# Moving the bias of the last feed-forward layer from TensorE rows to a GpSimd add, with all output tiles on VectorE

## The chip, the cores and the metric

The kernel runs on one core of one Trainium2 chip. The metric is the device time of one execution in microseconds (us). The engines are TensorE (PE, with its weight loads PEld), VectorE (DVE), ScalarE (ACT), GpSimd (POOL) and SyncE (SP), which here issues the DMAs. SBUF is the on-chip memory, PSUM the accumulator banks that TensorE writes.

## The reference

A sandwich ("macaron") transformer layer on x of 8 x 1024 tokens with 256 features:

```python
x = x + 0.5 * ffn(layernorm(x))
x = x + attention(layernorm(x))
x = x + 0.5 * ffn(layernorm(x))
```

The attention is causal with 16 heads of 16 features. The feed-forward layer has 8 nominal experts that share one weight matrix; since each token goes to two slots of them and none overflows, its part of that matrix product is scaled with the sum of the two renormalised top gates:

```python
scores = softmax(xf @ W_gate)                 # 7 gates
expert_weights, _ = top_k(scores, 2)
expert_weights = expert_weights / expert_weights.sum(-1, keepdims=True)
...
shared = xf @ W_shared.T
out = (shared + moe_out + bias).reshape(b, n, d)
```

## The kernel before, in words

Three stages follow one another. Stage A does the first feed-forward layer and the q, k, v projections, stage B the attention, and stage C (`stage_c`, from L1326), which is the one changed, everything after it: the division of the attention numerators by the softmax sums, the output projection, the residual, the layer norm, and the last feed-forward layer with its gates. Matrix products keep float32 accuracy by splitting both operands into a high and a low part: each product of 256 x 256 is six matmuls (high x high, high x low, low x high, for two halves of the 256 features), written by the helper `project` (L148, matmuls recorded at L152).

Stage C works on 16 chunks of 512 tokens, four tiles of 128 tokens in each. The engines are programmed apart, each with its own order written out by hand, and meet at semaphores. Each has a function `step(c, ...)`; steps 0 to 3 (and the last) are written out, the others run in loops of two chunks a turn (`turns`). In step c:

- **TensorE**: output projection of tile 0 of chunk c, the eight transposes of the normalised chunk c-1 (L247), output projection of tiles 1 to 3 (L152), then `pe_tile` four times for chunk c-1: expert columns and gate logits (264 columns, L152), then the shared weights (256 columns, L1240). Ahead of the latter, one matmul (L1237) of a constant matrix of twos with a row matrix holding the halved bias adds the bias into PSUM.
- **ScalarE**: the high half `xh` of chunk c-1 out of the transposes (L254), the exponentials of the gates of chunk c-2 (L1261), the high half `oh` of chunk c+1 (L1450), `yl` of tiles 0 to 2 of chunk c-1 (L1251: half the expert product, with the logits), the normalisation `xn` of chunk c (four instructions, L237), `yl` of tile 3, and the scaling of tiles 2 and 3 of chunk c-2 with the gate sum (`act_scale`, L1256).
- **VectorE**: `acc` of the second half of chunk c-2 (`dve_collect`, L1268: PSUM x 0.5 + residual), the logits (`lmax` L1276, `dl` L1277), the low half `xl` of chunk c-1 (L259), residual and statistics of chunk c (L1492, L210, L218), the gates of chunk c-2 (L1287 to L1295), output tiles 0 and 1 of chunk c-2 (`dve_outs`, L1306: yl x gate sum + acc), `acc` of the first half of chunk c-1.
- **GpSimd**: output tiles 2 and 3 of chunk c-3 (`pool_outs`, L1314), the low half `ol` of chunk c+1 (L1415), mean and inverse deviation of chunk c (L225 to L229), the division for chunk c+2 (L1410).
- **SyncE**: loads of numerators and inverse sums of chunk c+3 (L427, L434), the store of chunk c-3 (L1323), the load of the residual of chunk c+2 (L438).

An instruction that waits holds up everything behind it on its engine. Two buffers each (`acc`, `yl`, `out`, `x2`, `oh`, `ol`) alternate by the parity of the chunk. Ahead of the first step VectorE builds the bias row and the twos in five instructions (L1523 to L1527). Stage A adds its bias on GpSimd, a tile at a time (L365, `a_ffn_xb`).

Of the kernel before, what the change touches and what calls it, by code (L numbers as in the profile page):

```python
# [26 lines left out]
P = 128  # L27
# [1162 lines left out]
class Tail:  # L1190


    SPLIT = 2

    def __init__(self, ar, name, w, banks, ln, bias_w):
        self.w, self.banks, self.ln, self.bias_w = w, banks, ln, bias_w
        sb, sem = (lambda n, s, d=F32: ar.sb(f"{name}_{n}", s, d)), (lambda n: ar.sem(f"{name}_{n}"))
        self.acc = [sb(f"acc{n}", [P, TPC, E]) for n in range(2)]
# [16 lines left out]
        self.scaled = sem("scaled")  # L1215
        self.dve_out_done = sem("dve_out_done")
        self.pool_out_done = sem("pool_out_done")
        self.stored = [sem(f"stored{n}") for n in range(2)]

    def pe_tile(self, pe, k, t, first):  # L1220
# [23 lines left out]
    def act_tile(self, act, k, t, turn, fresh):  # L1244
        act.wait_ge(self.ex_done, k * TPC + t + 1)
        if not fresh:
            if t < self.SPLIT:
                act.wait_ge(self.dve_out_done, (k - 2) * 2 + t + 1)
            else:
                act.wait_ge(self.pool_out_done, (k - 2) * 2 + t - 1)  # L1250
        act.mul(self.yl[turn][:, t, :], self.banks["X"][t % 2][:, 0:YL], 0.5).then_inc(self.yl_ready, 1)  # L1251

    def act_scale(self, act, k, turn):
        act.wait_ge(self.gate_chain, k * GATE_LINKS + GATE_LINKS)
        for t in range(self.SPLIT, TPC):
            act.activation(self.yl[turn][:, t, 0:E], self.yl[turn][:, t, 0:E], ACT.Identity, scale=self.wsum[:, t:t + 1],  # L1256
                           bias=self.ln.zero[:, 0:1]).then_inc(self.scaled, 1)
# [21 lines left out]
    def dve_gate(self, dve, k, prev_scaled):  # L1279
# [3 lines left out]
        if prev_scaled:  # L1283
            dve.wait_ge(self.scaled, k * 2)
# [41 lines left out]
def stage_c(nc, psum, const, io, scratch, chunk):  # L1326
    ident, mhalf, zero, hbias, wh, wl, hold = const
    with ExitStack() as ctx:
# [14 lines left out]
        bh = ar.sb("c_bh", [P, E], F32R)  # L1343
        bl = ar.sb("c_bl", [P, E])
        bt = ar.sb("c_bt", [P, E])
        brow = ar.sb("c_brow", [P, E], F32R)
        twos = ar.sb("c_twos", [P, P], F32R)
        ln = Ffn(ar, "c_ln", (wh, wl), banks, zero)
        ffn = Tail(ar, "c_ffn", (wh, wl), banks, ln, (twos, brow))
# [7 lines left out]
        bias_chain = ar.sem("c_bias_chain")  # L1357
# [6 lines left out]
        def _(sp):  # L1364
# [8 lines left out]
            def step(c, parity, o_next, out3, x_next):  # L1373
# [23 lines left out]
            ffn.store(sp, io, LAST, LAST % 2, last=True)  # L1397
# [4 lines left out]
        def _(pool):  # L1402
# [237 lines left out]
```

## Time and profile before

| | before |
|---|---|
| time, median of 3 runs | 1353.83 us (1350.99 to 1354.71) |
| the profiled execution: time | 1353.6 us |
| its span | 1351.8 us |
| mean granted TensorE clock | 0.963 of full speed |
| PE busy | 1245.0 us, 92%, 9324 matmuls |
| DVE busy | 1138.3 us, 84% |
| ACT busy | 920.7 us, 68% |
| POOL busy | 435.0 us, 32% |
| last stage (L1403 to the end) | from 1150 us on, some 200 us |

Busy shares are averages over the whole program. A row of the timeline has a start, a duration, engine, line, operation, the output tile and the inputs with their shapes, a count of merged instructions, and in brackets the engine's idle time before it and what ended that. Merged rows cover all their instructions, which overlap a little at their ends: two of 1.29 us together may be 0.60 us apart.

### The profile page before, as it was taken

What the parts mean: (1) busy time and instruction counts of PE and PEld (TensorE: products, weight loads), DVE (VectorE), ACT (ScalarE), POOL (GpSimd) and SP (SyncE); (2) the same over time, 40 slices, a digit from 0 to 9 for tenths busy, and PEclk for the clock granted to TensorE, in tenths of its full rate; (3) what the DMA queues carried; (4) which work ended last, traced back from release to release, by engine and by line L of the source; (5) the groups of instructions that cost most, each with busy time, mean ns of one, the idle gap of its engine ahead of it and who ended that gap; (6) DMA issues with size and microseconds to landing.
All of it is one profiled execution on the core that took longest, in us unless ns stands there. A gap on an engine that the chain in (4) does not pass through costs nothing. (4 is left out here: it accounts for less than half of the span.)

```text
span 1351.8 us, 37753 instructions
## 1 busy us (share of the span) xinstructions
PE 1245.0 (92%) x9324; PEld 825.8 (61%) x9324; DVE 1138.3 (84%) x4510; ACT 920.7 (68%) x1858; POOL 435.0 (32%) x843
## 2 busy tenths in 40 slices
PE   4999999978999999999999999999999997699996
PEld 3988888964554454554554554554554543599996
DVE  4788888749999999999999999999999994367775
ACT  3666666630777777777777777777777777356654
POOL 3333333301222222222222222222322322467772
PEclk9999999985899999999999999999999999699998
DMA  3366666881564564664664664664664663556651
GB/s 113 141 225 225 225 225 225 220 274 37 78 107 81 99 106 80 101 104 80 103 102 80 103 102 80 104 101 80 106 99 80 106 99 107 158 180 196 192 165 63
DMA packets 121900, 174.12 MB, mean 129 GB/s; under 512 B 44012, under 2 KB 71788, under 8 KB 121804
## 3 DMA queue, kind: packets, MB, share of 16 engines
q1 hardware_dynamic: 121816, 173.30, 56.4%
q14 instruction: 67, 0.55, 0.2%
q8 instruction: 17, 0.28, 0.1%
HBM read 96.08 MB, written 76.02 MB: 127 GB/s over the span
## 5 line engine op out<-in xcount | busy, mean ns | idle before, releaser
L1000 ACT ACTIVATE b_probs<-bank 128x512 f32<-128x512 f32 x1152 | 597.4, 612 | 135.4 <-PE bank L1124 131.6
L1027 DVE CUSTOM_DVE_ANT_0 b_junk<-bank,mask 128x512 bf16<-128x512 f32 (+3 forms) x1032 | 446.8, 488 | 1.4 <-issue 1.2
L1030 DVE TENSOR_REDUCE b_pm<-bank 128x1 f32<-128x512 f32 x516 | 322.4, 683 | 19.7 <-PE bank L1101 18.7
L1143 PE MATMUL bank<-b_probs,b_vx 128*32 128x512 f32 (+3 forms) x3072 | 310.3, 499 | 4.2 <-ACT b_o L985 1.9
L1124 PE MATMUL bank<-qs,ks 50*128 50x512 f32 (+3 forms) x1056 | 293.6, 383 | 4.3 <-ACT b_probs L1000 0.4
L1101 PE MATMUL bank<-ks,qs 48*128 48x512 f32 (+3 forms) x1056 | 277.2, 390 | 10.9 <-PEq L443 6.3
L1101 PEld LDWEIGHTS bank<-ks,qs 48*128 48x128 f32 x1056 | 165.1, 193 | 134.6 <-DVE b_pm L1030 61.5
L145 POOL TENSOR_TENSOR hold_pool<-zero 128x1 f32<-128x1 f32 x192 | 37.4, 195 | 629.9 <-ACT b_probs L1000 474.3
L1124 PEld LDWEIGHTS bank<-qs,ks 50*128 50x128 f32 x1056 | 159.7, 188 | 57.3 <-ACT b_probs L1000 52.4
L960 POOL TENSOR_SCALAR_AFFINE_SELECT b_probs<-b_probs 128x512 f32<-128x512 f32 x256 | 158.5, 638 | 0.0
L1143 PEld LDWEIGHTS bank<-b_probs,b_vx 128*32 128x32 f32 x3072 | 71.1, 109 | 109.6 <-issue 80.9
L1124 PE MATMUL bank<-b_qs,b_ks 50*128 50x512 f32 (+2 forms) x480 | 135.3, 379 | 2.0
L1101 PE MATMUL bank<-b_ks,b_qs 48*128 48x512 f32 (+2 forms) x492 | 123.1, 371 | 2.0 <-DVE b_pm L1027 2.0
L152 PE MATMUL bank<-wh,a_ln_xh 128*128 128x256 f32 (+1 forms) x384 | 114.5, 298 | 6.1 <-DVE a_ln_xl L259 6.1
L152 PE MATMUL bank<-wh,a_ln_xl 128*128 128x256 f32 (+1 forms) x384 | 110.7, 288 | 0.0
L152 PE MATMUL bank<-wl,a_ln_xh 128*128 128x256 f32 (+1 forms) x384 | 110.3, 287 | 0.0
L1101 PEld LDWEIGHTS bank<-b_ks,b_qs 48*128 48x128 f32 x492 | 74.2, 185 | 56.9 <-DVE b_pm L1030 28.0
L1124 PEld LDWEIGHTS bank<-b_qs,b_ks 50*128 50x128 f32 x480 | 73.8, 185 | 24.5 <-ACT b_probs L1000 22.6
L237 ACT ACTIVATE a_ln_xn<-a_x,a_ln_nbias,a_ln_rstd 128x256 f32<-128x256 f32 x128 | 72.2, 591 | 21.8 <-POOL a_ln_nbias L229 21.3
L1027 DVE DVE_READ_ACCUMULATOR2_ANT b_pm<- 128x1 f32 x1032 | 85.7, 83 | 0.0
L152 PEld LDWEIGHTS bank<-wh,a_ln_xh 128*128 128x128 f32 x384 | 75.1, 196 | 10.5 <-DVE a_ln_xl L259 4.8
L152 PEld LDWEIGHTS bank<-wl,a_ln_xh 128*128 128x128 f32 x384 | 75.0, 195 | 0.8
(120 smaller groups left out, 1993.8 us busy)
## 6 DMA issues: line engine op xcount, KB each, us to landing
scr_qk<-a_qk SPq DMA_DIRECT2D x64, 512.0 KB, 3.2
qs<-scr_qk SPq DMA_DIRECT2D x132, 128.0 KB, 4.5
ks<-scr_qk SPq DMA_DIRECT2D x132, 128.0 KB, 5.1
scr_o<-b_o SPq DMA_DIRECT2D x64, 256.0 KB, 3.7
b_qs<-scr_qk SPq DMA_DIRECT2D x66, 128.0 KB, 4.0
b_ks<-scr_qk SPq DMA_DIRECT2D x66, 128.0 KB, 4.6
a_x<-x SPq DMA_DIRECT2D x16, 512.0 KB, 3.5
scr_x<-a_x SPq DMA_DIRECT2D x16, 512.0 KB, 2.7
```

What stands on the lines that cost most here:

```text
L145: pool.tensor_tensor(self.pool_out[:, col:col + 1], zero[:, 0:1], zero[:, 1:2], ALU.add)
L152: last = pe.matmul(out, a, b, start=(n == 0), stop=(n == len(terms) - 1))
L237: act.activation(self.xn[:, t, :], x[:, t, :], ACT.Identity, scale=self.rstd[:, t:t + 1], bias=self.nbias[:, t:t + 1]).then_inc(self.xn_re ...
L960: ins = pool.affine_select(out=blk, in_=blk, compare_op=ALU.is_ge, fill=0.0, base=0, pattern=[[0, GH], [1, P]], channel_multiplier=-1)
L1000: act.activation(probs[:, PROB_BUF[s], h, :], score_bank(g, t, last)[:], ACT.Exp).then_inc(p_ready, 1)
L1027: ins = dve.tensor_tensor_reduce(junk[:, t % MB, off:off + w], src, mask[:, BANK - w:BANK], 1.0, 0.0, ALU.add, ALU.max, pm[:, g.buf, 0, pl ...
L1030: ins = dve.tensor_reduce(pm[:, g.buf, 1, place(h), i:i + 1], src, AX.X, ALU.max)
L1101: last = pe.matmul(m_bank[t % MB][:, off:off + w], qs[g.buf][rows(h, SROWS), h // 2, i * P:(i + 1) * P], ks[g.buf][rows(h, SROWS), h // 2, ...
L1124: done = pe.matmul(score_bank(g, t, last)[:, off:off + w], ks[g.buf][rows(h, SROWS_M), h // 2, j * P:(j + 1) * P], qs[g.buf][rows(h, SROWS ...
L1143: last = pe.matmul(o_bank[2 * D * h:2 * D * (h + 1), col:col + w], vx[g.buf][:, j, h, :], probs[:, PROB_BUF[src], h, off:off + w], start=( ...
```

## The change

The bias is no longer a matmul. GpSimd adds the halved bias to the residual stream of the chunk, two instructions of two tiles each (`pool_xb`), in step c between the inverse deviation and the division; `acc` reads that sum in place of x2. VectorE writes all four output tiles of a chunk, each with its gate sum, so that ScalarE's scaling and GpSimd's two output adds are gone. The store of chunk c-2 comes in step c (before: c-3), behind the residual load. The bias rows, the twos and their five instructions are gone.

```diff
-    SPLIT = 2
-
-    def __init__(self, ar, name, w, banks, ln, bias_w):
-        self.w, self.banks, self.ln, self.bias_w = w, banks, ln, bias_w
+    def __init__(self, ar, name, w, banks, ln, hbias):
+        self.w, self.banks, self.ln, self.hbias = w, banks, ln, hbias
         sb, sem = (lambda n, s, d=F32: ar.sb(f"{name}_{n}", s, d)), (lambda n: ar.sem(f"{name}_{n}"))
+        self.xb = [sb(f"xb{n}", [P, TPC, E]) for n in range(2)]
...
-        half = sh[:, t % 2 * E:(t % 2 + 1) * E]
-        twos, brow = self.bias_w
-        pe.matmul(half, twos[:], brow[:], start=True, stop=False)
-        terms = [(a[ch], b[:, ch, cols]) for ch in range(KC) for a, b in ((lh, wh), (lh, wl), (ll, wh))]
-        for i, (a, b) in enumerate(terms):
-            last = pe.matmul(half, a, b, start=False, stop=(i == len(terms) - 1))
+        last = project(pe, sh[:, t % 2 * E:(t % 2 + 1) * E], lh, ll, [wh[:, ch, cols] for ch in range(KC)],
+                       [wl[:, ch, cols] for ch in range(KC)])
...
         if not fresh:
-            if t < self.SPLIT:
-                act.wait_ge(self.dve_out_done, (k - 2) * 2 + t + 1)
-            else:
-                act.wait_ge(self.pool_out_done, (k - 2) * 2 + t - 1)
+            act.wait_ge(self.out_done, (k - 2) * TPC + t + 1)
...
-    def act_scale(self, act, k, turn):
-        act.wait_ge(self.gate_chain, k * GATE_LINKS + GATE_LINKS)
-        for t in range(self.SPLIT, TPC):
-            act.activation(self.yl[turn][:, t, 0:E], self.yl[turn][:, t, 0:E], ACT.Identity, scale=self.wsum[:, t:t + 1],
-                           bias=self.ln.zero[:, 0:1]).then_inc(self.scaled, 1)
...
-    def dve_collect(self, dve, k, p, x, turn, fresh):
+    def pool_xb(self, pool, k, x, turn, fresh):
+        if not fresh:
+            pool.wait_ge(self.acc_ready, k * 2 - 2)
+        for p in range(2):
+            two = slice(2 * p, 2 * p + 2)
+            pool.tensor_tensor(self.xb[turn][:, two, :], x[:, two, :], self.hbias[:].unsqueeze(1).to_broadcast([P, 2, E]),
+                               ALU.add).then_inc(self.xb_ready, 1)
+
+    def dve_collect(self, dve, k, p, turn):
         dve.wait_ge(self.sh_done, k * 2 + p + 1)
-        if p == 1 and not fresh:
-            dve.wait_ge(self.pool_out_done, (k - 1) * 2)
+        dve.wait_ge(self.xb_ready, k * 2 + p + 1)
         two = slice(2 * p, 2 * p + 2)
         dve.scalar_tensor_tensor(out=self.acc[turn][:, two, :].rearrange("p t e -> p (t e)"), in0=self.banks["S"][p][:], scalar=0.5,
-                                 in1=x[:, two, :].rearrange("p t e -> p (t e)"), op0=ALU.mult,
+                                 in1=self.xb[turn][:, two, :].rearrange("p t e -> p (t e)"), op0=ALU.mult,
...
-        if prev_scaled:
-            dve.wait_ge(self.scaled, k * 2)
...
-    def dve_outs(self, dve, k, turn, fresh, tiles):
+    def dve_outs(self, dve, k, turn, fresh):
         self.out_free(dve, k, turn, fresh)
-        dve.wait_ge(self.acc_ready, k * 2 + (1 if tiles[-1] < 2 else 2))
-        for t in tiles:
+        dve.wait_ge(self.acc_ready, k * 2 + 2)
+        for t in range(TPC):
             dve.scalar_tensor_tensor(out=self.out[turn][:, t, :], in0=self.yl[turn][:, t, 0:E], scalar=self.wsum[:, t:t + 1],
-                                     in1=self.acc[turn][:, t, :], op0=ALU.mult, op1=ALU.add).then_inc(self.dve_out_done, 1)
-
-    def pool_outs(self, pool, k, turn, fresh):
-        self.out_free(pool, k, turn, fresh)
-        pool.wait_ge(self.acc_ready, k * 2 + 2)
-        for t in range(self.SPLIT, TPC):
-            pool.wait_ge(self.scaled, k * 2 + t - 1)
-            pool.tensor_tensor(self.out[turn][:, t, :], self.yl[turn][:, t, 0:E], self.acc[turn][:, t, :],
-                               ALU.add).then_inc(self.pool_out_done, 1)
-
-    def store(self, sp, io, k, turn, last=False):
-        if last:
-            sp.wait_ge(self.dve_out_done, k * 2 + TPC)
-        else:
-            sp.wait_ge(self.dve_out_done, k * 2 + 2)
-            sp.wait_ge(self.pool_out_done, k * 2 + 2)
+                                     in1=self.acc[turn][:, t, :], op0=ALU.mult, op1=ALU.add).then_inc(self.out_done, 1)
+
+    def store(self, sp, io, k, turn):
+        sp.wait_ge(self.out_done, k * TPC + TPC)
...
-            def step(c, parity, o_next, out3, x_next):
+            def step(c, parity, o_next, out2, x_next):
                 if o_next:
                     sp.wait_ge(on_ready, c * KC + 2 * KC)
                     load_o(c + 3, 1 - parity)
-                if out3:
-                    ffn.store(sp, io, c - 3, 1 - parity)
                 if x_next:
                     sp.wait_ge(x2_ready, c * 2 + 2)
                     load_x1(c + 2, parity)
+                if out2:
+                    ffn.store(sp, io, c - 2, parity)
...
-            def step(c, parity, out3, nxt, nxt2, first=False):
-                if out3:
-                    ffn.pool_outs(pool, c - 3, 1 - parity, isinstance(c, int) and c < 5)
+            def step(c, parity, nxt, nxt2, first=False):
                 if nxt:
                     low(c + 1, 1 - parity)
                 ln.pool_rstd(pool, c, mhalf, first)
+                ffn.pool_xb(pool, c, x2[parity], parity, isinstance(c, int) and c < 2)
                 if nxt2:
                     divide(c + 2, parity)
...
-                if prev2:
-                    ffn.act_scale(act, c - 2, parity)
...
-                    ffn.dve_gate(dve, c - 2, not young(3))
-                    ffn.dve_outs(dve, c - 2, parity, young(4), (0, 1))
-                if prev:
-                    ffn.dve_collect(dve, c - 1, 0, x2[turn], turn, young(3))
+                    ffn.dve_gate(dve, c - 2)
+                    ffn.dve_outs(dve, c - 2, parity, young(4))
+                if prev:
+                    ffn.dve_collect(dve, c - 1, 0, turn)
...
-            bias = Chain(dve, bias_chain, 0)
-            bias(dve.tensor_scalar(bh[:], hbias[:], 1.0, None, ALU.mult))
-            bias(dve.tensor_tensor(bl[:], hbias[:], bh[:].bitcast(F32), ALU.subtract))
-            bias(dve.tensor_scalar(bt[:], bh[:].bitcast(F32), ident[:, 0:1], None, ALU.mult))
-            bias(dve.scalar_tensor_tensor(out=brow[:], in0=bl[:], scalar=ident[:, 1:2], in1=bt[:], op0=ALU.mult, op1=ALU.add))
-            bias(dve.tensor_scalar(twos[:], ident[:], 0.0, 2.0, ALU.mult, ALU.add))
...
-                    if first:
-                        pe.wait_ge(bias_chain, 5)
```

**Orders before and after.** VectorE ahead of its loop, from the gates' sum (`wsum`) of one chunk to the low half of another. Before:

```order
L1295 TENSOR_TENSOR c_ffn_wsum<-c_ffn_w 128x4
L1306 SCALAR_TENSOR_TENSOR c_ffn_out<-c_ffn_yl,c_ffn_wsum,c_ffn_acc 128x256 x2
L1268 SCALAR_TENSOR_TENSOR c_ffn_acc<-bank,c_x 128x512 x2
L1276 TENSOR_REDUCE c_ffn_lmax<-c_ffn_yl 128x4
L1277 TENSOR_TENSOR c_ffn_dl<-c_ffn_yl,c_ffn_lmax 128x28
L259 TENSOR_TENSOR c_ln_xl<-bank,c_ln_xh 128x512 x2
L1492 TENSOR_TENSOR c_x<-bank,c_x 128x512
```

and with the change (L1296 is the output tile, L1260 `acc`, L1268 and L1269 are `lmax` and `dl`):

```order
L1285 TENSOR_TENSOR c_ffn_wsum<-c_ffn_w 128x4
L1296 SCALAR_TENSOR_TENSOR c_ffn_out<-c_ffn_yl,c_ffn_wsum,c_ffn_acc 128x256 x4
L1260 SCALAR_TENSOR_TENSOR c_ffn_acc<-bank,c_ffn_xb 128x512 x2
L1268 TENSOR_REDUCE c_ffn_lmax<-c_ffn_yl 128x4
L1269 TENSOR_TENSOR c_ffn_dl<-c_ffn_yl,c_ffn_lmax 128x28
L259 TENSOR_TENSOR c_ln_xl<-bank,c_ln_xh 128x512 x2
L1455 TENSOR_TENSOR c_x<-bank,c_x 128x512
```

Four output tiles stand where two stood, ahead of the two `acc`, and `acc` reads `c_ffn_xb`.

GpSimd ahead of its loop, from the inverse deviation to the low half `c_ol` of the next chunk. Before:

```order
L228 TENSOR_TENSOR c_ln_rstd<-c_ln_veps,mhalf 128x4
L229 TENSOR_TENSOR c_ln_nbias<-c_ln_nmean,c_ln_rstd 128x4
L1410 TENSOR_TENSOR on<-c_num,c_rden 128x512 x2
L1314 TENSOR_TENSOR c_ffn_out<-c_ffn_yl,c_ffn_acc 128x256 x2
L1415 TENSOR_TENSOR c_ol<-on,c_oh 128x512 x2
```

and with the change (L1253 adds the bias, L1382 divides, L1387 is the low half):

```order
L228 TENSOR_TENSOR c_ln_rstd<-c_ln_veps,mhalf 128x4
L229 TENSOR_TENSOR c_ln_nbias<-c_ln_nmean,c_ln_rstd 128x4
L1253 TENSOR_TENSOR c_ffn_xb<-c_x,hbias 128x512 x2
L1382 TENSOR_TENSOR on<-num,rden 128x512 x2
L1387 TENSOR_TENSOR c_ol<-on,c_oh 128x512 x2
```

The two adds of 512 columns are ahead of the divides; the output adds of 256 columns behind them are gone.

## Rows read from the trace of the kernel before

**Rows 1.** The page, busy time of each engine over the span.

```profile
PE 1245.0 (92%) x9324; PEld 825.8 (61%) x9324; DVE 1138.3 (84%) x4510; ACT 920.7 (68%) x1858; POOL 435.0 (32%) x843
```

**Rows 2.** Last stage in slices: stretch, then busy us per engine, clock, DMA.

```profile
1260.00:1280.00 20.00, 19.30 (x160) 18.89 (x160) 14.97 (x54) 12.10 (x29) 15.77 (x20) 1.00 0.70 195
```

**Rows 3.** One step on TensorE: start, us, engine, line, operation, idle before.

```profile
1273.15 0.38 PE L152 MATMUL bank<-wh,c_ln_xh 128*128 128x264 f32 x1 [0.35 <-DVE c_ln_xl L259]
...
1274.00 0.28 PE L1237 MATMUL bank<-c_brow,c_twos 128*128 128x256 f32 x1
1274.12 0.28 PE L1240 MATMUL bank<-wh,c_ln_xh 128*128 128x256 f32 x1
```

**Rows 4.** The same step on VectorE, in order of time.

```profile
1271.60 1.29 DVE L259 TENSOR_TENSOR c_ln_xl<-bank,c_ln_xh 128x512 fp32r<-128x512 f32 x2 [1.05 <-ACT c_ln_xh L254]
...
1275.84 0.38 DVE L218 BATCH_NORM_AGGREGATE c_ln_mv<-c_ln_stats 128x2 f32<-128x6 f32 x4
...
1277.01 0.17 DVE L1294 TENSOR_TENSOR c_ffn_w<-c_ffn_top,c_ffn_rden 128x8 f32<-128x8 f32 x1
...
1277.65 0.88 DVE L1306 SCALAR_TENSOR_TENSOR c_ffn_out<-c_ffn_yl,c_ffn_wsum,c_ffn_acc 128x256 f32<-128x256 f32 x2 [0.28 <-DVE c_ffn_wsum L1295]
1278.45 0.68 DVE L1268 SCALAR_TENSOR_TENSOR c_ffn_acc<-bank,c_x 128x512 f32<-128x512 f32 x1
...
1280.72 0.18 DVE L1276 TENSOR_REDUCE c_ffn_lmax<-c_ffn_yl 128x4 f32<-128x28 f32 x1 [0.21 <-ACT c_ffn_yl L1251]
1280.93 0.19 DVE L1277 TENSOR_TENSOR c_ffn_dl<-c_ffn_yl,c_ffn_lmax 128x28 f32<-128x28 f32 x1
1282.17 1.29 DVE L259 TENSOR_TENSOR c_ln_xl<-bank,c_ln_xh 128x512 fp32r<-128x512 f32 x2 [1.05 <-ACT c_ln_xh L254]
```

**Rows 5.** The chain of waits in the step: start, us, what.

```profile
1270.11 0.22 ACT c_ffn_yl L1256
...
1271.00 0.58 ACT c_ln_xh L254
```

**Rows 6.** The same step on GpSimd, in order of time.

```profile
1272.76 2.53 POOL L1415 TENSOR_TENSOR c_ol<-on,c_oh 128x512 fp32r<-128x512 f32 x2 [0.64 <-ACT c_oh L1450]
1276.40 0.20 POOL L225 TENSOR_TENSOR c_ln_nmean<-zero,c_ln_mv 128x4 f32<-128x4 f32 x1 [1.10 <-DVE c_ln_mv L218]
...
1276.87 1.04 POOL L228 TENSOR_TENSOR c_ln_rstd<-c_ln_veps,mhalf 128x4 f32<-128x4 f32 x1
...
1278.20 2.74 POOL L1410 TENSOR_TENSOR on<-num,rden 128x512 f32<-128x512 f32 x2
```

**Rows 7.** The same step on ScalarE, in order of time.

```profile
1278.33 2.08 ACT L237 ACTIVATE c_ln_xn<-c_x,c_ln_nbias,c_ln_rstd 128x256 f32<-128x256 f32 x4 [0.53 <-POOL c_ln_nbias L229]
...
1281.57 1.05 ACT L254 CAST c_ln_xh<-bank 128x512 fp32r<-128x512 f32 x2
```

**Rows 8.** GpSimd in steps 3 and 4 of the last stage.

```profile
1203.98 2.54 POOL L1410 TENSOR_TENSOR on<-c_num,c_rden 128x512 f32<-128x512 f32 x2
...
1214.48 0.31 POOL L229 TENSOR_TENSOR c_ln_nbias<-c_ln_nmean,c_ln_rstd 128x4 f32<-128x4 f32 x1
1214.74 2.78 POOL L1410 TENSOR_TENSOR on<-num,rden 128x512 f32<-128x512 f32 x2
```

**Rows 9.** Durations in ns (min/median/max) of two lines; GpSimd in the first stage.

```profile
L345 DVE TENSOR_TENSOR a_ffn_den<-a_ffn_top x16: 166/650/664, 27.2 to 275.7; 128x4 f32<-128x4 f32 x16
...
L1292 DVE TENSOR_TENSOR c_ffn_den<-c_ffn_top x16: 165/169/173, 1188.2 to 1345.9; 128x4 f32<-128x4 f32 x16
...
108.38 2.82 POOL L365 TENSOR_TENSOR a_ffn_xb<-a_x,hbias 128x256 f32<-128x256 f32 x4
```

**Rows 10.** VectorE in step 4 of the last stage.

```profile
1214.24 0.88 DVE L1306 SCALAR_TENSOR_TENSOR c_ffn_out<-c_ffn_yl,c_ffn_wsum,c_ffn_acc 128x256 f32<-128x256 f32 x2 [0.28 <-DVE c_ffn_wsum L1295]
```

**Rows 11.** TensorE near the end: stretch, busy us and count, granted clock, DMA.

```profile
1334.00:1336.00 2.00, 0.38 (x2) 0.94 0.04 8
1336.00:1338.00 2.00, 1.67 (x7) 0.50 0.73 248
```

More of the change, by code:

```diff
@@ L1214, in __init__ @@
         self.ex_ready = sem("ex_ready")
-        self.scaled = sem("scaled")
-        self.dve_out_done = sem("dve_out_done")
-        self.pool_out_done = sem("pool_out_done")
+        self.xb_ready = sem("xb_ready")
+        self.out_done = sem("out_done")
         self.stored = [sem(f"stored{n}") for n in range(2)]
@@ L1277, in dve_logits, with dve_gate @@
         ch(dve.tensor_tensor(self.dl[:], logits, self.lmax[:].unsqueeze(2).to_broadcast([P, TPC, NEXP]), ALU.subtract))
-    def dve_gate(self, dve, k, prev_scaled):
+    def dve_gate(self, dve, k):
         ch = Chain(dve, self.gate_chain, k * GATE_LINKS)
@@ L1342, in stage_c @@
         x2 = [ar.sb(f"c_x2{n}", [P, TPC, E]) for n in range(2)]
[L1343 to L1347, printed above, removed]
         ln = Ffn(ar, "c_ln", (wh, wl), banks, zero)
-        ffn = Tail(ar, "c_ffn", (wh, wl), banks, ln, (twos, brow))
+        ffn = Tail(ar, "c_ffn", (wh, wl), banks, ln, hbias)
         den_loaded = ar.sem("c_den_loaded")
@@ L1390, in _ @@
             sp.wait_ge(r_stored, 16)
-            for c in range(3):
+            for c in range(2):
                 step(c, c % 2, True, False, True)
+            step(2, 0, True, True, True)
             turns(sp, 3, NCHUNK - 3, lambda c, parity: step(c, parity, True, True, True))
@@ L1396, in _ @@
                 step(c, c % 2, False, True, False)
-            ffn.store(sp, io, LAST, LAST % 2, last=True)
             for turn in range(2):
@@ L1429, in _ @@
             divide(1, 1)
-            step(0, 0, False, True, True, True)
-            step(1, 1, False, True, True)
-            step(2, 0, False, True, True)
-            step(3, 1, True, True, True)
-            step(4, 0, True, True, True)
-            turns(pool, 5, NCHUNK - 2, lambda c, parity: step(c, parity, True, True, True))
-            step(NCHUNK - 2, 0, True, True, False)
-            step(LAST, 1, True, False, False)
-            for c in (LAST + 1, LAST + 2):
-                ffn.pool_outs(pool, c - 3, (c - 3) % 2, False)
+            step(0, 0, True, True, True)
+            step(1, 1, True, True)
+            turns(pool, 2, NCHUNK - 2, lambda c, parity: step(c, parity, True, True))
+            step(NCHUNK - 2, 0, True, False)
+            step(LAST, 1, False, False)
         @block.scalar
@@ L1503, in step @@
                 if prev2:
-                    ffn.dve_collect(dve, c - 2, 1, x2[parity], parity, young(4))
+                    ffn.dve_collect(dve, c - 2, 1, parity)
                     ffn.dve_logits(dve, c - 2, parity)
@@ L1535, in _ @@
             step(NCHUNK, 0, True, True, False)
-            ffn.dve_collect(dve, LAST, 1, x2[1], 1, False)
+            ffn.dve_collect(dve, LAST, 1, 1)
             ffn.dve_logits(dve, LAST, 1)
-            ffn.dve_gate(dve, LAST, True)
-            ffn.dve_outs(dve, LAST, 1, False, range(TPC))
+            ffn.dve_gate(dve, LAST)
+            ffn.dve_outs(dve, LAST, 1, False)
         @block.tensor
```

1 line of the change is left out of this document (removed).

## The prediction

> **What bounds the kernel now.** I read the engine totals, the last stage in slices of 20 us, the chain of waits, and then one step of the stage on each engine, in order of time. The totals [rows 1] suggest TensorE (92%), and so does a slice of the last stage: 19.30 of 20 us, at the full clock [rows 2]. That is the wrong reading here. TensorE stands idle 0.35 us in each step until VectorE has written the low half `c_ln_xl` [rows 3], and that instruction starts 10.57 us after its predecessor, at 1282.17 after 1271.60 [rows 4]. The chain runs through the small engines [rows 5] and closes on itself, piece by piece:
>
> - VectorE, from xl to the end of the last aggregate: 1275.84 + 0.38 - 1271.60 = 4.62 us [rows 4];
> - to GpSimd 0.18, its four small instructions 1276.40 to 1278.20: 1.80 [rows 6];
> - to ScalarE 0.13, four normalisations 2.08 [rows 7];
> - from their end (1280.41) to the high half `c_ln_xh` at 1281.57: 1.16. This is the fourth `yl` and the two scalings at L1256, queued ahead of xh on ScalarE [rows 5, 7];
> - to the next xl 0.60 [rows 4, 7]. Sum 10.57, the whole step. VectorE idles 1.05 us ahead of xl.
>
> **The change, part by part.** All sums are against the profiled execution (1353.6 us; median of the runs 1353.83).
>
> *TensorE loses four bias matmuls per chunk.* One takes 0.12 us of the queue (1274.00 to 1274.12) [rows 3], so 0.48 per step. TensorE isn't what ends the step, so it waits longer instead: nothing, save after the last chunk, where no step follows: -0.5 us.
>
> *ScalarE loses the two scalings.* They lie on the chain. Without them xh waits for the transposes only. No row at full clock shows that alone; bounds are 0 (transposes hidden) and 1.16 (nothing gained). Taking 0.57, about half a microsecond for a matmul, its end and the hand-over, the step could be 10.57 - 1.16 + 0.57 = 9.98 us. That is the gain on offer.
>
> *The five bias-building instructions on VectorE and the constants go:* nothing; the first chunks wait for a load that lands after them.
>
> *GpSimd: two 256-column adds go, two of 512 columns come, between `nbias` and the divides.* The trace has no 512-column add of this form; the divides beside it take 2.54 for two where nothing disturbs them [rows 8], so 1.27 each. Upper bound: four 256-column adds of a bias, 2.82 for four [rows 9], 1.41 per 512 columns. GpSimd's own sum is then 2.53 (low halves) + 1.80 + 2.54 + 2.54 = 9.41 us, under 9.98: by count alone it fits. The GPSIMD Engine Reference, section on elementwise cycle accounting, has 4497 ns for a 2048-column add, an estimate of 1.12 us for 512; the measured divides say 1.27, and by the page's figure the total below would be some 4 us smaller.
>
> *VectorE writes four output tiles in place of two,* 0.40 each (two from 1277.65 to 1278.45) [rows 4]: 0.80, against 1.05 idle. By count it fits as well.
>
> *What does not fit is that the two meet.* An output tile reads two SBUF tensors (`yl`, `acc`). Three places show such a VectorE instruction and a GpSimd one keeping each other out. In the first stage the tiny `den` takes a median 650 ns while GpSimd adds the bias, 169 ns in the last stage, where nothing runs against it [rows 9]; the four adds end at 111.20, and it ends with the fourth. In step 4 of the last stage `nbias` starts 0.24 after the first output tile, takes 0.31 (a like instruction takes 0.20 [rows 6]), so it gets in between the two tiles, which start 0.40 apart; the divide behind it is held until the second tile is through, and the pair takes 2.78 in place of 2.54 [rows 8, 10]. So whoever waits gets in at the other's next boundary. Instructions that take one input from PSUM (xl, acc, the residual) pay nothing. The Trainium skill, SBUF — State Buffer, "Who interferes with whom", has the same pairing, but lets the holder keep the ports "for the whole instruction". Here `w2`, with two SBUF inputs, takes its usual 0.17 inside GpSimd's 1.04 us power instruction [rows 4, 6]; so a long instruction on four columns blocks nobody, and the trace decides. By the page's words the outputs would start some 0.3 us later in both kernels, and the difference would stay.
>
> Before, two tiles met GpSimd once, for 0.24 us, off the chain. Now GpSimd comes with four long SBUF readers just as VectorE starts four outputs. Per step:
>
> - xl to the first output, 1277.65 - 1271.60: 6.05;
> - two outputs, before the first add can get in: 0.80;
> - from there they alternate: add 1.27, output 0.40, add 1.27, output 0.40;
> - first divide 1.27. Beside it VectorE does both `acc` (PSUM input, free; 0.60 each, as two xl of that size take 0.60 + 0.69) and `lmax` (1280.72 to 1280.93, 0.21) [rows 4]: 1.41, so it comes to `dl` (two SBUF inputs) 0.14 us after the second divide has started, and waits for that too: 1.27. Behind `dl` stands xl.
>
> That is 6.05 + 0.80 + 4 x 1.27 + 2 x 0.40 = 12.73; each of the three GpSimd instructions that wait behind an output hides about 0.06 of its start (the held divide lost 0.24 where the tile had 0.30 left), so 12.55 us, +1.98 over 10.57. ScalarE and TensorE are early: xh ends some 2 us before `dl`.
>
> Steps 4 to 13 (the loops, with divides): 10 x 1.98 = 19.8. Steps 14 and 15 have adds but no divides: 6.05 + 0.80 + 2 x 1.27 + 0.80 - 0.12 + 1.41 + 0.19 = 11.67, +1.1 each, 2.2. Steps 2 and 3 stand ahead of the loops; there the outputs start 0.28 sooner (no idle ahead of them), a third gets through, and three GpSimd instructions are waited for: about 11.0, +0.5 each, 1.0. The end -0.5. Sum +22.5: **1376 us**.
>
> *TensorE will idle about 3 us per step.* Where it idled 1.61 us behind scattered transposes, its granted clock fell to 0.50 (1.2 GHz) for about 2 us [rows 11]; a dozen matmuls at 0.22 instead of 0.12 would be 1.4 us. The 2 us by which xh is early cover it; without that cover it would add up to 1.4 x 12 = 17 us.
>
> *SyncE's queue:* each store moves behind the `x1` load and waits for VectorE's fourth output of chunk c-2; the next numerator loads stand behind it. Those are needed a step and a half later and land in about 7 us: nothing. Were the cover gone, a divide would wait a few us per step. The new waits on the adds ahead of `acc` cost nothing, as the adds ran a step earlier.
>
> **Rivals.** (a) *The blocks are fewer.* `dl` slips in ahead of the second divide (0.14 us is thin), or a third output passes before the first add: three GpSimd instructions instead of four, 12.55 - 1.27 = 11.28, +0.71 x 10 + 2.2 + 1.0 - 0.5 = +9.8: 1363.5 us. For it: margins of 0.1 to 0.3 us decide. Against: the instruction behind `nbias` starts 0.50 to 0.55 us after the first output in either step shown [rows 4, 6, 8, 10], and only before 0.40 or after 0.80 would the order change.
>
> (b) *No blocking by these adds.* `hbias` is broadcast from 256 columns, and wide instructions on both engines have met only briefly so far. If they share, the step is 9.98 from step 2 on: 14 x -0.59 - 0.5 = -8.8: 1344.8 us, faster. It decides if the outputs keep 0.48 us each beside GpSimd's adds. Against it: the 650 ns of `den`, whose opponent in the first stage is this very kind of add, from the same `hbias` [rows 9].
>
> (c) *They lock into an order that costs two blocks.* 12.55 - 2.54 = 10.0, and with remnants 10.3 to 10.8, eating the gain of the scalings: 1350 to 1358 us.
>
> **How the numbers follow.** Four blocks 0.56, (a) 0.24, (c) 0.08, (b) 0.12. About 0.3% (4 us) is what a measurement can tell from no change. Slower: 0.56 + 0.24 + 0.02 of (c) = 0.82; same 0.06; faster 0.12. The likeliest case alone is 1368 to 1382: 1.41 us per add (+0.28 x 12 = 3.4, a bit more with delays) on top, some steps with three blocks below. The whole range takes in (a) and leaves out (b) and most of (c): 1357 to 1382.
>
> **What would show it.** Right: output tiles three and four at about 1.5 us each on VectorE where the first two keep 0.48; `dl` about 1.2 us in place of 0.19; step 12.5 us; adds and first divide each 0.2 to 0.3 us longer than 1.27; xn to xh down from 1.16 to about 0.5; TensorE idle near 3 us per step, waiting for xl. Wrong: outputs at 0.48 throughout (rival b), `dl` at 0.19 with one slow output (rival a), or TensorE without idle time.

## The result, and the profile after

The changed kernel takes 1374.65 us (median of 4 runs, 1369.99 to 1377.74) against 1352.41 us for the kernel before on the same chip (4 runs, 1349.70 to 1354.71): a ratio of 1.0162, 95% interval 1.0126 to 1.0199. It is slower, by 22 us. The forecast was 1376.0 us.

The profiled execution of the changed kernel is the fastest of its four, 1369.99 us with a span of 1368.2. Its last stage also began early: the first division there starts at 1158.19, against 1161.08 in the kernel before. In the ten other profiled kernels of this case, all with the same first two stages, this start lies anywhere from 1156.52 to 1164.48. So I compare steps of the stage, not ends.

The page has the busy time of each engine and, by engine, the chain of work that ended last:

```profile
PE 1243.2 (91%) x9260; PEld 823.2 (60%) x9260; DVE 1183.1 (86%) x4535; ACT 909.8 (66%) x1828; POOL 456.8 (33%) x845
...
DVE 8%; PE 3%; issue 2%; DVEq 1%; DMA 1%; POOL 1%; ACT 0%; SPq 0%; POOLq 0%
```

VectorE is 44.8 us busier than before [rows 1], far more than the 30 output tiles it took over would cost at 0.40 each (12.0). One step on VectorE shows why (timeline, in order of time):

```profile
1254.76 1.29 DVE L259 TENSOR_TENSOR c_ln_xl<-bank,c_ln_xh 128x512 fp32r<-128x512 f32 x2 [0.15 <-DVE c_ffn_dl L1269]
...
1260.75 3.75 DVE L1296 SCALAR_TENSOR_TENSOR c_ffn_out<-c_ffn_yl,c_ffn_wsum,c_ffn_acc 128x256 f32<-128x256 f32 x4 [0.28 <-DVE c_ffn_wsum L1285]
1264.43 1.27 DVE L1260 SCALAR_TENSOR_TENSOR c_ffn_acc<-bank,c_ffn_xb 128x512 f32<-128x512 f32 x2
1265.63 0.17 DVE L1268 TENSOR_REDUCE c_ffn_lmax<-c_ffn_yl 128x4 f32<-128x28 f32 x1
1265.83 1.10 DVE L1269 TENSOR_TENSOR c_ffn_dl<-c_ffn_yl,c_ffn_lmax 128x28 f32<-128x28 f32 x1
1267.09 1.29 DVE L259 TENSOR_TENSOR c_ln_xl<-bank,c_ln_xh 128x512 fp32r<-128x512 f32 x2 [0.15 <-DVE c_ffn_dl L1269]
```

The step is 12.33 us from `xl` to `xl`, against 10.57 [rows 4]. The four output tiles take 3.75 us together; two took 0.88. `dl`, on 28 columns, takes 1.10; it took 0.19. VectorE idles only in small gaps of 0.15 to 0.28 us: the time stands inside the instructions. The third tile by itself, from a narrower stretch of the same view (the fourth takes 1.51, the first two 0.48 each):

```profile
1261.55 1.52 DVE L1296 SCALAR_TENSOR_TENSOR c_ffn_out<-c_ffn_yl,c_ffn_wsum,c_ffn_acc 128x256 f32<-128x256 f32 x1
```

The same step on GpSimd:

```profile
1261.16 0.20 POOL L229 TENSOR_TENSOR c_ln_nbias<-c_ln_nmean,c_ln_rstd 128x4 f32<-128x4 f32 x1
1261.31 2.91 POOL L1253 TENSOR_TENSOR c_ffn_xb<-c_x,hbias 128x512 f32<-128x512 f32 x2
1264.18 2.72 POOL L1382 TENSOR_TENSOR on<-num,rden 128x512 f32<-128x512 f32 x2
1267.86 2.52 POOL L1387 TENSOR_TENSOR c_ol<-on,c_oh 128x512 fp32r<-128x512 f32 x2 [0.97 <-ACT c_oh L1416]
```

Two adds take 2.91 and two divides 2.72, where the undisturbed pair takes 2.54 [rows 8]. The second divide ends at 1266.90 and `dl` at 1266.93: `dl` ends with the divide that it waited for. So three instructions of VectorE are held, tiles three and four and `dl`. Over all steps, in ns (minimum, median, maximum):

```profile
L1296 DVE SCALAR_TENSOR_TENSOR c_ffn_out<-c_ffn_yl,c_ffn_wsum,c_ffn_acc x64: 475/485/1535, 1185.3 to 1364.3; 128x256 f32<-128x256 f32 x64
...
L1269 DVE TENSOR_TENSOR c_ffn_dl<-c_ffn_yl,c_ffn_lmax x16: 186/1106/1126, 1178.7 to 1361.3; 128x28 f32<-128x28 f32 x16
```

ScalarE in the next step (timeline):

```profile
1273.82 2.08 ACT L237 ACTIVATE c_ln_xn<-c_x,c_ln_nbias,c_ln_rstd 128x256 f32<-128x256 f32 x4 [0.79 <-POOL c_ln_nbias L229]
...
1276.32 1.08 ACT L254 CAST c_ln_xh<-bank 128x512 fp32r<-128x512 f32 x2
1279.31 0.23 ACT L1246 ACTIVATE c_ffn_ex<-c_ffn_dl 128x28 f32<-128x28 f32 x1 [1.91 <-DVE c_ffn_dl L1269]
```

From the end of `xn` (1275.90) to `xh` it is now 0.42 us, where it was 1.16 [rows 7] (0.83 in the step before this one, where TensorE ran at a lower clock, as shown below). `xh` is ready early and ScalarE then waits 1.91 us for `dl`. TensorE waits as well: a slice of 20 us, then slices of 2 us behind two of its idle times (columns as in [rows 2]), then what it waited for from 1220 to 1320 us (total, times, longest):

```profile
1230.00:1250.00 20.00, 16.64 (x135) 15.94 (x135) 18.37 (x55) 9.28 (x21) 14.84 (x17) 1.00 0.60 157
```

```profile
1244.00:1246.00 2.00, 2.00 (x16) 2.00 (x17) 1.93 (x5) 0.39 (x1) 1.73 (x2) 1.00 0.39 134
...
1254.00:1256.00 2.00, 0.18 (x2) 0.00 (x0) 1.84 (x4) 1.33 (x3) 1.03 (x2) 1.00 0.44 144
1256.00:1258.00 2.00, 1.69 (x11) 1.70 (x12) 1.97 (x5) 0.39 (x1) 2.00 (x2) 0.79 0.33 111
1258.00:1260.00 2.00, 2.00 (x11) 2.00 (x11) 1.72 (x15) 0.00 (x0) 0.46 (x3) 0.50 0.52 170
```

```profile
PE bank L152 <- DVE c_ln_xl L259: 13.8, 8, 2.1
```

TensorE now idles 3.4 us in this slice (0.70 before) and 14.7 of the 100 us from 1210 to 1310, 1.8 per step. After the idle time of 2.1 us from 1254.2 to 1256.3 its granted clock goes down to 0.50 (1.2 GHz), from 1257.1 to 1260.6; in the next step the idle time is 1.05 us and the clock stays at 1.00. But it also stays at 1.00 after the 2.1 us from 1241.9 to 1244.0. From 1217 to 1331 us there are ten such waits for `xl`, six of 2.1 us and four of 1.05 to 1.09. The clock falls behind four of the six, for 3.4 us each, and behind none of the four, each of which is the next one after a fall. So of the slices of 20 us from 1210 to 1310 three show 0.91 and two 1.00, where all from 1210 to 1330 showed 1.00 before.

**The whole difference, stretch by stretch,** from the starts of `xl` in the two traces: first step to step 4, 37.26 us against 37.13 (+0.1); steps 4 to 13, 1205.42 to 1328.81 against 1208.19 to 1313.89 (+17.7); steps 14 and 15, 22.68 against 21.10 (+1.6); the end, 13.32 against 13.41 (-0.1). That is +19.3; with the start of the stage 2.9 us earlier it is the 16.4 us between the two spans. The +19.3 lies inside the interval of the ratio (17 to 27 us).

### The profile page after: what moved, and what is told of

It is laid out like the page before. It is cut to its first block and busy times, and to the rows that moved or that the text cites. A ratio compares the mean times of both kernels' runs of the same rounds, so it can differ in the third digit from the quotient of the medians.

```text
span 1368.2 us, 37601 instructions
## 1 busy us (share of the span) xinstructions
PE 1243.2 (91%) x9260; PEld 823.2 (60%) x9260; DVE 1183.1 (86%) x4535; ACT 909.8 (66%) x1828; POOL 456.8 (33%) x845
## 5 line engine op out<-in xcount | busy, mean ns | idle before, releaser
L1101 PE MATMUL bank<-ks,qs 48*128 48x512 f32 (+3 forms) x1056 | 278.0, 391 | 10.8 <-PEq L443 6.3
L152 PE MATMUL bank<-wh,c_ln_xh 128*128 128x264 f32 (+1 forms) x256 | 77.3, 302 | 21.9 <-DVE c_ln_xl L259 21.9
L152 PEld LDWEIGHTS bank<-wh,a_ln_xh 128*128 128x128 f32 x384 | 74.8, 195 | 10.3 <-DVE a_ln_xl L259 4.8
```

Of the source, the lines that this page charges most:

```text
L152: last = pe.matmul(out, a, b, start=(n == 0), stop=(n == len(terms) - 1))
L1101: last = pe.matmul(m_bank[t % MB][:, off:off + w], qs[g.buf][rows(h, SROWS), h // 2, i * P:(i + 1) * P], ks[g.buf][rows(h, SROWS), h // 2, ...
```

## The experiments

The theory: an instruction of VectorE that reads two SBUF tensors and one of GpSimd that reads two keep each other out, and whichever waits gets in at the other's next boundary. Four GpSimd instructions in a row, with two output tiles let in between them, then make the step; on VectorE three instructions are held, two tiles and `dl`. I call the wait of one held instruction a hold. Rivals: GpSimd's mere load or its writes into SBUF slow VectorE; the adds' place in the order does it; VectorE's four tiles are too much by themselves; the removed parts (bias rows, scalings) were worth something else than I said. All ratios are to the kernel before, run beside each experiment, with 95% intervals. "The first divide" and so on are GpSimd's, and the output tiles are VectorE's unless it says otherwise.

### The adds as pure writes

```diff
+        self.ln.hold.pool(pool, 3, self.ln.zero)
...
-            pool.tensor_tensor(self.xb[turn][:, two, :], x[:, two, :], self.hbias[:].unsqueeze(1).to_broadcast([P, 2, E]),
-                               ALU.add).then_inc(self.xb_ready, 1)
+            half = self.xb[turn][:, two, :].rearrange("p t e -> p (t e)")
+            pool.memset(half, 0.0).then_inc(self.xb_ready, 1)
+            pool.memset(self.junk[:, p, 0:2 * E], 0.0)
+            pool.memset(self.junk[:, p, 2 * E:3 * E], 0.0)
```

The first line of the diff is an add of one column that stands ahead of the six fills (`hold_pool` below); `junk` is a buffer that nothing reads.

> The changed kernel with the two bias adds of a step replaced by GpSimd fills of about the same length (512 + 512 + 256 columns each), which write SBUF and read nothing; the residual and the bias are left out of acc. If the time is lost because VectorE's output tiles and GpSimd instructions that read SBUF keep each other out, only the divides are left to meet: a step of 10.3 to 11.5 us in place of 12.34, output tiles 3 and 4 held at most once by a divide, 1350 to 1362 us. If the loss is GpSimd's load or its order (2.5 us more between nbias and the divides), nothing changes: 12.3 us a step, 1374.

Measured: 1352.44 us, ratio 1.0011 (0.9993 to 1.0028). The step is 10.76 us. VectorE beside the fills, then GpSimd (timelines):

```profile
1246.48 1.68 DVE L1300 SCALAR_TENSOR_TENSOR c_ffn_out<-c_ffn_yl,c_ffn_wsum,c_ffn_acc 128x256 f32<-128x256 f32 x4 [0.28 <-DVE c_ffn_wsum L1289]
...
1249.82 1.27 DVE L1273 TENSOR_TENSOR c_ffn_dl<-c_ffn_yl,c_ffn_lmax 128x28 f32<-128x28 f32 x1
```

```profile
1247.04 0.38 POOL L145 TENSOR_TENSOR hold_pool<-zero 128x1 f32<-128x1 f32 x1
1247.36 0.52 POOL L1256 MEMSET c_ffn_xb<- 128x512 f32 x1
...
1249.47 0.31 POOL L1258 MEMSET c_ffn_junk<- 128x256 f32 x1
1249.75 2.55 POOL L1386 TENSOR_TENSOR on<-c_num,c_rden 128x512 f32<-128x512 f32 x2
```

GpSimd is as busy in the same place, 2.7 us from 1247.04 to 1249.75, and writes more than the adds did (2560 columns against 1024); the four tiles take 1.68 us, as long as where nothing runs against them (1.67 in the next experiment). Load and writes are out as a cause. The divide behind the fills reads two tensors, and it holds `dl` at once: 1.27.

### The adds wait for the output tiles

```diff
             pool.wait_ge(self.acc_ready, k * 2 - 2)
+            pool.wait_ge(self.out_done, k * TPC - TPC)
```

> The changed kernel with one wait more: GpSimd starts the bias adds of a step only when all four output tiles of that step are written. Mutual exclusion: the outputs go through at 0.40 us each, the adds run beside acc, only dl is held; a step of 10.5 to 10.8 us, 1352 to 1357 us, so an added wait makes it some 20 us faster. If VectorE's load, or the length of GpSimd's row of work, is the cause: no gain, or slower still, since GpSimd now starts 1.1 us later in each step (1374 to 1390).

Measured: 1353.18 us, ratio 1.0007 (0.9989 to 1.0025). One more wait and nothing else makes the changed kernel some 21 us faster. The step is 10.49. VectorE and GpSimd:

```profile
1252.79 1.67 DVE L1297 SCALAR_TENSOR_TENSOR c_ffn_out<-c_ffn_yl,c_ffn_wsum,c_ffn_acc 128x256 f32<-128x256 f32 x4 [0.28 <-DVE c_ffn_wsum L1286]
...
1256.14 0.98 DVE L1270 TENSOR_TENSOR c_ffn_dl<-c_ffn_yl,c_ffn_lmax 128x28 f32<-128x28 f32 x1
```

```profile
1254.54 2.54 POOL L1254 TENSOR_TENSOR c_ffn_xb<-c_x,hbias 128x512 f32<-128x512 f32 x2 [1.14 <-DVE c_ffn_out L1297]
1257.03 2.55 POOL L1383 TENSOR_TENSOR on<-num,rden 128x512 f32<-128x512 f32 x2
1259.51 2.58 POOL L1388 TENSOR_TENSOR c_ol<-on,c_oh 128x512 fp32r<-128x512 f32 x2
```

GpSimd idles 1.14 us and still comes out ahead, because its long instructions then run at their undisturbed 1.27 or close to it. So four output tiles aren't too much for VectorE by themselves. The only hold left is `dl` behind the second add, and the step closes over it: output tiles to adds 1.75 us, the two adds 2.54, from there to `xl` 0.20, `xl` to the output tiles 6.00; together 10.49.

### The order turned round: divides first

```diff
-                ffn.pool_xb(pool, c, x2[parity], parity, isinstance(c, int) and c < 2)
                 if nxt2:
                     divide(c + 2, parity)
+                ffn.pool_xb(pool, c, x2[parity], parity, isinstance(c, int) and c < 2)
```

> The changed kernel with GpSimd's two adds behind the two divides instead of ahead of them. Four long SBUF readers follow nbias as before, only in another order. Mutual exclusion: outputs 3 and 4 are held by the divides, dl by the second add; step 12.2 to 12.6, 1372 to 1378 us, as the change. If what costs is that the divides come 2.5 us later (late numerators, late high and low halves), the time falls to 1350 to 1360.

Measured: 1371.82 us, ratio 1.0161 (1.0127 to 1.0195), step 12.33: the changed kernel again. VectorE, then GpSimd:

```profile
1252.18 3.72 DVE L1296 SCALAR_TENSOR_TENSOR c_ffn_out<-c_ffn_yl,c_ffn_wsum,c_ffn_acc 128x256 f32<-128x256 f32 x4 [0.28 <-DVE c_ffn_wsum L1285]
...
1257.23 1.12 DVE L1269 TENSOR_TENSOR c_ffn_dl<-c_ffn_yl,c_ffn_lmax 128x28 f32<-128x28 f32 x1
```

```profile
1252.80 2.82 POOL L1382 TENSOR_TENSOR on<-c_num,c_rden 128x512 f32<-128x512 f32 x2
1255.59 2.71 POOL L1253 TENSOR_TENSOR c_ffn_xb<-c_x,hbias 128x512 f32<-128x512 f32 x2
```

The output tiles take 3.72 us beside divides and `dl` 1.12 beside an add. It isn't something in the adds, or in `hbias` being broadcast.

### The bias in TensorE's rows, four tiles on VectorE

The changed kernel without `pool_xb`: the bias rows and the five building instructions are back, `acc` reads the residual itself.

> The changed kernel with the bias back in TensorE rows and no adds on GpSimd; VectorE writes all four tiles, ScalarE scales nothing. Mutual exclusion: the outputs now meet the two divides in the adds' place, two of them are held for 1.2 us each: a step of 11.3 to 11.6 us, 1357 to 1361 us. If only the adds do the harm, the gain of the scalings shows alone: a step of 10.0, 1344.

Measured: 1355.09 us, ratio 1.0055 (1.0034 to 1.0076), a little under the forecast. Step 11.41. VectorE:

```profile
1253.47 3.75 DVE L1290 SCALAR_TENSOR_TENSOR c_ffn_out<-c_ffn_yl,c_ffn_wsum,c_ffn_acc 128x256 f32<-128x256 f32 x4 [0.28 <-DVE c_ffn_wsum L1279]
1257.14 1.27 DVE L1254 SCALAR_TENSOR_TENSOR c_ffn_acc<-bank,c_x 128x512 f32<-128x512 f32 x2
1258.34 0.17 DVE L1262 TENSOR_REDUCE c_ffn_lmax<-c_ffn_yl 128x4 f32<-128x28 f32 x1
1258.54 0.19 DVE L1263 TENSOR_TENSOR c_ffn_dl<-c_ffn_yl,c_ffn_lmax 128x28 f32<-128x28 f32 x1
```

With two long readers left on GpSimd there are two holds inside the tiles and none at `dl`. So 0.92 us of the changed kernel's 12.33 belongs to the adds, as they push the second divide onto `dl`; the two holds inside the tiles would be there without any add, only by VectorE's writing tiles while GpSimd divides.

### The adds cut in four

```diff
-        for p in range(2):
-            two = slice(2 * p, 2 * p + 2)
-            pool.tensor_tensor(self.xb[turn][:, two, :], x[:, two, :], self.hbias[:].unsqueeze(1).to_broadcast([P, 2, E]),
-                               ALU.add).then_inc(self.xb_ready, 1)
+        for t in range(TPC):
+            last = pool.tensor_tensor(self.xb[turn][:, t, :], x[:, t, :], self.hbias[:], ALU.add)
+            if t % 2 == 1:
+                last.then_inc(self.xb_ready, 1)
```

> The changed kernel with its two adds of 512 columns cut into four of 256 (0.72 us each undisturbed, 0.3 us more work per step in sum). Mutual exclusion: outputs 3 and 4 are held for about 0.65 us each instead of 1.1, and dl arrives with the first divide, not the second: step 11.0 to 11.9 us, 1359 to 1369 us. If the load of GpSimd is the cause, 0.3 us per step more: 1378.

Measured: 1364.35 us, ratio 1.0100 (1.0069 to 1.0132), step 11.39. The same work in shorter pieces:

```profile
1252.38 2.66 DVE L1296 SCALAR_TENSOR_TENSOR c_ffn_out<-c_ffn_yl,c_ffn_wsum,c_ffn_acc 128x256 f32<-128x256 f32 x4 [0.28 <-DVE c_ffn_wsum L1285]
...
1256.36 1.26 DVE L1269 TENSOR_TENSOR c_ffn_dl<-c_ffn_yl,c_ffn_lmax 128x28 f32<-128x28 f32 x1
```

The tiles lose 0.99 us here (2.66 less 1.67) and 2.08 beside the long adds: half the length of the adds, half the loss. `dl` now meets the first divide just as it starts, and loses all of it.

### What the removed parts were worth

Without the bias rows (the kernel before less L1237's matmul; the bias is left out of the output):

> The kernel before without its four bias matmuls per chunk (the bias is left out). If TensorE's queue does not end the step, nothing: 1352 us, within 1.5 us of before, TensorE idling 0.8 us per step. If TensorE were the bound, 16 x 0.48 = 7.7 us less, 1345.

Measured: 1350.76 us, ratio 1.0001 (0.9985 to 1.0017), step 10.57 with the same 1.05 us of idle ahead of `xl`. Taking TensorE's 64 instructions out bought nothing.

Without the scalings (the kernel before less `act_scale`; the factor left out of output tiles 2 and 3 is the sum of the two gates, which are normalised to one, so it changes them by rounding only):

> The kernel before without ScalarE's two scalings per chunk (the gate factor is left out of output tiles 3 and 4); GpSimd still writes these two. If the scalings lie on the chain xn, yl, scale, xh, xl, the step falls from 10.57 to about 10.0 us and the time by 6 to 9 us, to 1344 to 1347. If TensorE or something else ends the step, less than 2 us.

Measured: 1344.51 us, ratio 0.9957 (0.9936 to 0.9978). The gain on offer is real. The step is 10.18, not 9.98; VectorE at its end:

```profile
1253.64 0.67 DVE L1277 TENSOR_TENSOR c_ffn_dl<-c_ffn_yl,c_ffn_lmax 128x28 f32<-128x28 f32 x1
1254.47 1.29 DVE L259 TENSOR_TENSOR c_ln_xl<-bank,c_ln_xh 128x512 fp32r<-128x512 f32 x2 [0.15 <-DVE c_ffn_dl L1277]
```

```profile
1250.90 2.67 POOL L1408 TENSOR_TENSOR on<-num,rden 128x512 f32<-128x512 f32 x2
1253.53 1.44 POOL L1312 TENSOR_TENSOR c_ffn_out<-c_ffn_yl,c_ffn_acc 128x256 f32<-128x256 f32 x2
```

As soon as the loop is shorter, `dl` slides into GpSimd's output tiles and is held 0.48 us by the first of them, which ends with it.

### A version without holds

The bias in TensorE's rows, four tiles on VectorE, and each divide of GpSimd behind what it would hold, the first behind the tiles, the second behind `dl` (from chunk 4 on):

```diff
+                if not (isinstance(c, int) and c < 4):
+                    pool.wait_ge(ffn.out_done, c * TPC - 3 * TPC)
                 for ch in range(KC):
+                    if ch == 1 and not (isinstance(c, int) and c < 4):
+                        pool.wait_ge(ffn.gate_chain, c * GATE_LINKS - 3 * GATE_LINKS + 2)
```

> As rows_four_outs, with two waits more on GpSimd: the first divide of a step starts when the four outputs are written, the second when dl is done. Nothing with two SBUF inputs then meets a long GpSimd instruction. Mutual exclusion: outputs and dl undisturbed, step 10.0 us, 1343 to 1347 us, faster than both kernels. If lateness of GpSimd's work is what costs, the two waits make it slower than rows_four_outs.

Measured: 1345.51 us, ratio 0.9970 (0.9951 to 0.9989): faster than both kernels. Step 9.95. VectorE, GpSimd, and the slice:

```profile
1254.73 1.67 DVE L1290 SCALAR_TENSOR_TENSOR c_ffn_out<-c_ffn_yl,c_ffn_wsum,c_ffn_acc 128x256 f32<-128x256 f32 x4 [0.28 <-DVE c_ffn_wsum L1279]
...
1258.08 0.19 DVE L1263 TENSOR_TENSOR c_ffn_dl<-c_ffn_yl,c_ffn_lmax 128x28 f32<-128x28 f32 x1
1258.69 0.69 DVE L259 TENSOR_TENSOR c_ln_xl<-bank,c_ln_xh 128x512 fp32r<-128x512 f32 x1 [0.42 <-ACT c_ln_xh L254]
```

```profile
1256.49 1.29 POOL L1386 TENSOR_TENSOR on<-num,rden 128x512 f32<-128x512 f32 x1 [1.14 <-DVE c_ffn_out L1290]
1258.35 1.30 POOL L1386 TENSOR_TENSOR on<-num,rden 128x512 f32<-128x512 f32 x1 [0.56 <-DVE c_ffn_dl L1263]
```

```profile
1240.00:1260.00 20.00, 20.00 (x171) 20.00 (x171) 17.25 (x62) 11.63 (x27) 13.66 (x17) 1.00 0.63 216
```

No hold is left, and TensorE shows no idle time. Of the 6.2 us that ten steps gain, 3.5 are given back in two steps ahead of them, where the stage is still filling (13.55 and 11.37 us, against 10.84 and 10.57): VectorE comes late to `dl` there, and the second divide waits for it. So do the rows of the bias count at last? The same kernel without them (bias left out of the output):

> rows_guarded without the four bias matmuls per chunk; the bias is left out of the output. In rows_guarded a slice of the last stage has TensorE busy 20.00 of 20 us at the full clock, and the step is 9.95 us. If TensorE's rows are what ends that step (my theory), the 4 x 0.12 = 0.48 us of rows come off it until the small engines bind: VectorE idles 0.42 us ahead of the low half xl there, so the step falls to about 9.5 us, ten to twelve steps give 4.5 to 5.5 us, and the time is some 1340 us, a ratio to before of 0.993 to 0.994. Rival: the loop through the small engines (aggregate, GpSimd's four small instructions, normalisation, transposes, xh, xl) already ends the 9.95 us step and TensorE's queue is only nearly full; then the step stays at 9.9 to 9.95, the ratio at 0.997, and the rows are worth nothing even there, as in no_bias_rows (1.0001).

Measured: 1345.73 us, ratio 0.9949 (0.9930 to 0.9967; the two kernels' intervals overlap). The step is 9.85, so neither expectation is met: of the 0.48 us of rows 0.10 comes off, then the loop through the small engines binds again, with `xl` still waiting for `xh`:

```profile
1247.16 1.29 DVE L259 TENSOR_TENSOR c_ln_xl<-bank,c_ln_xh 128x512 fp32r<-128x512 f32 x2 [0.33 <-ACT c_ln_xh L254]
```

The two limits were within 0.1 us of each other, and a busy count of 20.00 of 20 didn't say how near the second one was. In the two traces even this 0.10 is not kept: ten steps take 1.0 us less than in rows_guarded, and two steps ahead of them 1.0 us more (15.01 and 10.91 against 13.55 and 11.37); no run explains these early steps.

The kernel before took 1350.39 to 1353.26 us beside these runs, so the ratios are to be compared, not the times.

| kernel | time, us | ratio to before | step, us |
|---|---|---|---|
| changed kernel | 1374.65 | 1.0162 | 12.33 |
| adds_behind_divides | 1371.82 | 1.0161 | 12.33 |
| four_short_adds | 1364.35 | 1.0100 | 11.39 |
| rows_four_outs | 1355.09 | 1.0055 | 11.41 |
| guard_adds | 1353.18 | 1.0007 | 10.49 |
| fill_only | 1352.44 | 1.0011 | 10.76 |
| no_bias_rows | 1350.76 | 1.0001 | 10.57 |
| guarded_no_rows | 1345.73 | 0.9949 | 9.85 |
| rows_guarded | 1345.51 | 0.9970 | 9.95 |
| no_scaling | 1344.51 | 0.9957 | 10.18 |

## Why the prediction was right

By its own steps:

- **What bounds the kernel.** Right. The loop over the small engines, not TensorE with its 92%: taking 64 matmuls away moved nothing (no_bias_rows), taking two small ScalarE instructions per chunk away moved 0.43%, some 6 us (no_scaling).
- **The step without holds, 9.98 us.** Nearly right. The gap from `xn` to `xh` was put at 0.57 and is 0.42 in the changed kernel at the full clock; the loop free of holds and of bias rows is 9.85 (guarded_no_rows). But I gave that figure to the change as "the gain on offer" without asking where `dl` would then stand. In no_scaling it is 10.18, as `dl` meets a GpSimd instruction.
- **The add at 1.27 us each.** Right: 2.54 for two where nothing disturbs them (guard_adds). The upper bound, 1.41, and the estimate of 1.12 from the Trainium skill's page (GPSIMD Engine Reference, elementwise cycle accounting) are both off.
- **Mutual exclusion, alternation at boundaries, four blocks.** Right in kind and number: four GpSimd instructions with two tiles between them, and `dl` behind the last. The tiles grew by 3.75 - 1.67 = 2.08 and `dl` by 0.91. The rivals fell with the trace: no blocking (b) or three blocks (a) by the two slow tiles and the slow `dl` of every step from 4 to 13, an order with two (c) by 12.33 us against its 10.3 to 10.8. One that I had not named, load or writes of GpSimd, fell with the fills.
- **The size, +1.98 per step.** A little high: +1.77. From `xl` to the first output it is 5.99 instead of 6.05, and from there to the next `xl` 6.34 instead of 6.50. Two errors partly cancel in the latter. From the first output to the end of `dl` it is 6.18 us (1260.75 to 1266.93): counted from end to end, a held tile costs 0.28 or 0.29 behind the add before it, where I had 0.40, and each of the first three GpSimd instructions 1.15 behind the tile before it, where I had 1.21. And from the end of `dl` to `xl` it is 0.16, for which the sum had no term. Ten steps give 17.7 instead of 19.8.
- **Steps 2 and 3, +0.5 each, and 14 and 15, +1.1 each.** The first pair measured +0.28 and +0.59, with 2.73 us for the four tiles of 1185.34, so one hold fewer, as forecast; the second pair +1.6 together. The interval ahead of them is 0.74 us shorter than before (11.58 against 12.32), which I had not forecast and no run explains; in the other nine kernels it is anything from 10.56 to 12.31. Without it the sum would be +20.0. Nor had I seen the hold of the very first `dl` (1178.69, 1.01 us).
- **The end, -0.5.** It is -0.1, and no run says where the rest of the tail goes.
- **TensorE's idle time and clock.** Near 3 us per step was forecast, 1.8 measured. I had left out what a slower clock does to it: four of the ten steps spend some 1.5 us more on the same matmuls (`yl` 2.60 and 1.77 us apart on ScalarE, 1.44 each at the full clock), close to the 1.4 that I had worked out from [rows 11]. The 2 us of lower clock that I read there were one slice; in both traces it lasts 3.4 us, in the kernel before from 1335.8 to 1339.2. The cover held: `xh` then ends 0.8 us before `dl` instead of 1.9, and both kinds of step are 12.33 us.
- **SyncE's queue and the new waits.** Nothing, as forecast: no wait for a DMA stands in the steps.

The nearness of 1374.65 to 1376.0 is partly luck. By the trace the sum is +19.3, not +22.5; the median of four runs happens to lie 3 us higher.

## What to carry to other kernels

Busy counts per engine say whether work fits, not whether it fits at the same moment: before moving work to GpSimd, mark on both timelines where each engine reads two SBUF tensors, and count GpSimd's boundaries between VectorE's instructions. The cure for such holds is a wait on the engine with slack, so that its long readers start behind the other's short ones (12.33 to 10.49 us per step for one line), or pieces that are shorter (11.39). And when a loop gets shorter, look again at which instructions now meet.

## What the runs showed of the hardware

- GpSimd's fills of 512 columns (0.47 us from start to start) read nothing, and they leave VectorE's two-tensor reads alone though both engines write SBUF: 1.68 us for four tiles. Every long GpSimd instruction that held something here reads two SBUF tensors; what one with a single input does, no run shows.
- The waiting engine gets in at every boundary, in both directions and in each kernel, with either order of adds and divides: in the last stage of all eleven traces no output tile and no `dl` waits past the end of one long GpSimd instruction, and none of those waits past the end of one tile or `dl`. The recorded durations contain the wait: `dl`, on 28 columns, shows 0.19, 0.67, 0.98, 1.10 or 1.27 us, by how much was left of GpSimd's instruction.
- TensorE's granted clock fell behind four of the six idle times of 2.1 us from 1217 to 1331 us in the changed kernel (four of six in adds_behind_divides too), and behind none of 1.05 to 1.12 us in these two kernels, nor of the ten of 1.17 to 1.19 us in four_short_adds. So an idle time of that length alone doesn't decide it, and the kinds of step don't simply take turns.
